# Attention loop of a four-layer kernel: up products into the ring's banks, a halved down product, a partition exchange for the rotation, and one exponential over four banks per quad

## The reference

```
xn = layernorm(x);  q = l2norm(xn @ Wq);  k = l2norm(xn @ Wk);  v = xn @ Wv
clock = softplus(xn @ clock_w + clock_b)
q = rope(q, times);  k = rope(k, times)      # r1 = x1*cos - x2*sin, r2 = x1*sin + x2*cos on channel pairs
gcp = exp(clip(cumsum(-softplus(xn @ gate_w + gate_b)), -60, 50))
q = q * gcp;  k = k / (gcp + 1e-8)
p = xn @ p_w + p_b;  p_exp = exp(p - max(p)) * clock
q = q / (cumsum(p_exp) + 1e-8);  k = k * p_exp
attn = softmax(causal(q k^T / sqrt(8)));  out = attn @ v @ out_w + out_b
x1 = out + residual;  h = layernorm(x1)
return x1 + gelu(h @ mlp_w1 + mlp_b1) @ mlp_w2 + mlp_b2
```

## Time and profile before

| what | us |
|---|---|
| median of 3 runs | 2212.62 |
| span of the profiled execution, first to last instruction | 2164.4 |
| median less span, outside the instructions | 48.2 |
| start to the first up product of step 3 | 102.7 |
| 13 steps with all parts, 41.83 each (to 646.4) | 544 |
| from 646.4 on: steps 16 to 18, then the experts, the scan and the rotation, which the change doesn't touch | 1518 |

### The profile page before, as it was taken

How to read it: one execution, slowest core, us unless ns; L and a number is a source line. 1 busy time by engine, 2 the same in 40 slices (tenths; PEclk the granted TensorE clock), 3 DMA queues, 4 the chain that set the end, 5 groups by cost and what they waited for, 6 DMA issues and landing times. The chain is left out here.

```text
span 2164.4 us, 37241 instructions
## 1 busy us (share of the span) xinstructions
PE 1849.2 (85%) x12576; PEld 954.5 (44%) x12600; DVE 1703.8 (79%) x3547; ACT 1474.7 (68%) x2917; POOL 1165.1 (54%) x720
## 2 busy tenths in 40 slices
PE   6999999999998459957889889898898988659996
PEld 2566666656665259952222222222222222124453
DVE  7778868877863437854899999999999998976776
ACT  5888888888885138845656666666666666437775
POOL 2122232242221027871789999999999998840001
PEclk9999999999999669977899999999999998879998
DMA  4100010011001012221100111001111100023333
GB/s 169 36 26 26 28 49 26 26 36 41 21 25 33 20 50 77 88 72 42 30 25 27 34 35 34 27 30 30 31 35 35 35 31 30 21 67 90 97 84 78
DMA packets 103708, 97.35 MB, mean 45 GB/s; under 512 B 9137, under 2 KB 86113, under 8 KB 103137
## 3 DMA queue, kind: packets, MB, share of 16 engines
q1 hardware_dynamic: 95584, 75.34, 12.4%
q0 software_dynamic: 6784, 18.10, 2.5%
q10 hardware_dynamic: 1152, 1.54, 0.2%
HBM read 45.87 MB, written 28.10 MB: 34 GB/s over the span
## 5 line engine op out<-in xcount | busy, mean ns | idle before, releaser
L1935 POOL TENSOR_TENSOR hc<-h,c_rep 128x1024 f32<-128x1024 f32 x256 | 627.8, 2463 | 137.9 <-DVE h L1899 136.7
L1899 DVE TENSOR_TENSOR_SCAN h<-decay,bank 128x1024 f32<-128x1024 f32 x241 | 551.0, 2286 | 22.5 <-issue 0.9
L1757 ACT ACTIVATE decay<-bank,neg_a_r 128x510 f32<-128x510 f32 x512 | 322.6, 683 | 257.5 <-PE bank L1634 257.1
L1618 PE MATMUL bank<-u_in,sel_rows 32*128 32x512 f32 x964 | 287.9, 675 | 95.7 <-DVE h L1899 95.6
L1634 PE MATMUL bank<-delta,sel_rows 32*128 32x512 f32 x1024 | 338.8, 677 | 0.9 <-ACT decay L1757 0.9
L1886 DVE TENSOR_TENSOR bank<-bank,b_rep 128x1024 f32<-128x1024 f32 x241 | 291.2, 1208 | 34.8 <-PE bank L1618 33.0
L992 POOL DMA_INDIRECT rows_in_dram<-row,idx x64 | 63.3, 989 | 318.3 <-DVE row L965 303.7
L574 ACT ACTIVATE es<-bank 128x384 f32<-128x384 f32 x512 | 208.9, 499 | 22.1 <-PE bank L373 21.8
L1618 PEld LDWEIGHTS bank<-u_in,sel_rows 32*128 32x128 f32 x964 | 76.0, 191 | 276.7 <-DVE h L1899 199.7
L1649 PE MATMUL bank<-hc,y_sel 128*32 128x512 f32 x1024 | 149.6, 660 | 0.8 <-POOL hc L1935 0.8
L1656 PE MATMUL bank<-xpad,w_conv 128*128 128x512 f32 x256 | 133.0, 634 | 3.2 <-ACT xc L1819 1.6
(11 more groups left out here) (341 smaller groups left out, 4170.0 us busy)
## 6 DMA issues: line engine op xcount, KB each, us to landing
r_tw<-r_o_t SPq DMA_DIRECT2D x96, 128.0 KB, 2.3
xvs<-xv SPq DMA_DIRECT2D x16, 512.0 KB, 2.9
u_wide<-u_rep_dram SPq DMA_DIRECT2D x30, 256.0 KB, 3.5
xs<-rows_in_dram SPq DMA_DIRECT2D x72, 68.0 KB, 1.8
front<-in_x_dram SPq DMA_DIRECT2D x16, 256.0 KB, 2.9
w<-in_w_dram SPq DMA_DIRECT2D x2, 2048.0 KB
xlb_dram<-front SPq DMA_DIRECT2D x16, 256.0 KB, 2.3
xlb_m<-xlb_dram SPq DMA_DIRECT2D x16, 256.0 KB
```

The costliest lines, as they stand in the source:

```text
L1618: last = pe.matmul(BD[n % 2][:, i * STEP:(i + 1) * STEP], sel[at:at + 32, r, :], u_in[p if n < NS else q][at:at + 32, hf, :], start=True, ...
L1757: act.activation(decay[n % 4][:, i, :, 1:], seq(DL[i])[:, :, 1:], ACT.Exp, scale=c["neg_a_r"][:, hf, g:g + 1]).then_inc(s["n_da"], 1)
L1899: dve.tensor_tensor_scan(flat(h[n % RING]), decay[n % 4].rearrange("p i b t -> p (i b t)"), flat(drive_0) if by_pool else BD[n % 2], 0.0, ...
L1935: pool.tensor_tensor(hc[n % RING][:, :, :], h[n % RING][:, :, :], c_rep[p if n < NS else q][:, :].unsqueeze(1).to_broadcast([P, 2, STEP]), ...
```

## The change

- **Up products.** `up(n)` writes bank n of the ring instead of M, and the four are issued together, behind exponential 5 of the pair at work. Quad 6 waits until all four Gelus have read the banks.
- **Down product.** It is cut in two halves of two token tiles: one ahead of quad 7, one behind weighing 6. x2 waits for the second. Weighing 7 moves behind quad 0.
- **Partition exchange.** w_qs and w_ks and their products are gone. VectorE multiplies q itself with the (signed) sine into rot_b, SP sends rot_b to rot_s with even and odd partitions swapped (`swap`, two transfers of 64 partitions), and rot minus rot_s replaces rot plus rot_b. For k the same, through the same two tiles.
- **One exponential.** `exps(n)` is one instruction over the four banks, [128 x 4 x 384], behind the last mask addition; s_score counts one for each quad.
- **Order.** On TensorE `back(3)` moves behind quad 1, `weigh(1)` behind quad 2, the transposes of xl2 and the router's product later. On ScalarE `av_copy(3)` moves behind exponential 0, `av_copy(0)` behind exponential 2, and the copy of x2t behind it. On VectorE both products of q's rotation stand ahead of x2, and the router's small steps behind `heads_o(0)`. GpSimd's L985 also waits for m_xl2.
- Start: the weights w_a come in three transfers, without the two swapped ones. `of` and `before` lie in log.

```diff
+        def swap(sp, sem):
+            for to in range(2):
+                sp.dma_start(rot_s[to:P:2, :], rot_b[1 - to:P:2, :]).then_inc(sem, 16)
...
+                sp.wait_ge(s["f_rb"], one_on)
+                swap(sp, s["f_qsw"])
+                sp.wait_ge(s["f_kb"], one_on)
+                sp.wait_ge(s["f_rq"], one_on)
+                swap(sp, s["f_ksw"])
...
-                pe.matmul(M[:, :], c["w_up"][:, n * P:(n + 1) * P], h_t[:, :], start=True, stop=True).then_inc(s["m_up"], 1)
+                pe.matmul(RING[n], c["w_up"][:, n * P:(n + 1) * P], h_t[:, :], start=True, stop=True).then_inc(s["m_up"], 1)
...
-                for st in range(HS):
-                    act.wait_ge(s["s_score"], u * 32 + HS * n + st + 1)
-                    if st == 0:
-                        since(act, s["s_av"], u * 8 + n - 1)
-                    last = act.activation(es[(n % 2) * HS + st][:, :], RING[st][:, 0:3 * P], ACT.Exp, scale=DH ** -0.5)
-                last.then_inc(s["s_exp"], 1)
+                act.wait_ge(s["s_score"], u * 8 + n + 1)
+                since(act, s["s_av"], u * 8 + n - 1)
+                act.activation(es[n % 2][:, :, :], ring[:, :, 0:3 * P], ACT.Exp, scale=DH ** -0.5).then_inc(s["s_exp"], 1)
...
+                since(dve, s["f_ksw"], 32 * k)
+                dve.tensor_tensor(seq(rot_b), seq(FA), sin, ALU.mult).then_inc(s["f_rb"], 1)
...
+                dve.wait_ge(s["f_qsw"], 32 * k + 32)
+                dve.tensor_tensor(rot[:, :], rot[:, :], rot_s[:, :], ALU.subtract).then_inc(s["f_rq"], 1)
...
                 pool.wait_ge(s["f_back"], k + 1)
+                if tail:
+                    pool.wait_ge(s["m_xl2"], k - 2)
                 pool.tensor_tensor(mag[:, 1, :], mag[:, 1, :], one_up[:, :], ALU.subtract).then_inc(s["f_lost"], 1)
```

More of the change, by code:

```diff
@@ L137, in program @@
         for name, width in W_A:
+            if name in ("w_qs", "w_ks"):
+                continue
             c[name] = c["w_a"][:, at:at + width]
@@ L165, in split3, with attention @@
     chain(dve.tensor_copy(dst[96:96 + rows], rest))
-def attention(nc, dram, d, c, banks):
+def attention(nc, dram, d, c, psum, banks):
     with ExitStack() as ctx:
@@ L275, in attention @@
         end = sb("end", [1, E])
-        of = sb("of", [1, ETILES])
-        before = sb("before", [1, ETILES])
+        of, before = (log[0:1, 0, n * ETILES:(n + 1) * ETILES] for n in range(2))
         hi = sb("p_hi", [E * FC, P], bf16)
@@ L432, in pe_step @@
                 pe.wait_ge(s["m_ht_sb"], k - 2)
-                up(0)
+                pe.wait_ge(s["s_exp"], 8 * (k - 2) + 6 if late else 8 * PAIRS)
+                for n in range(FC):
+                    up(n)
             if front:
@@ L457, in pe_step @@
                 pe.wait_ge(s["m_gelu"], 4 * k - 8)
[L458 to L462 removed]
+                down(range(0, 2))
             if late:
                 quad(7, k - 2, p)
+                weigh(6, k - 2, p)
+            if tail:
+                down(range(2, TS))
             if front:
[L466 to L470 removed]
+                pe.wait_ge(s["f_sq"], k + 1)
+                pe.wait_ge(s["f_rb"], k + 1)
+                pe.matmul(FA[:, :], c["ones_blk"], square[:, :], start=True, stop=True).then_inc(s["f_ssq"], 1)
             if k == 1:
@@ L490, in pe_step @@
                 quad(1, k - 1, q)
-            if front:
-                pe.wait_ge(s["f_mq"], k + 1)
-                project(FA, c["w_ks"], s["f_ks"])
+            if late:
+                back(3, k - 2)
             if scores:
                 weigh(0, k - 1, q)
+            if scores:
+                quad(2, k - 1, q)
+                weigh(1, k - 1, q)
             if tail:
@@ L500, in pe_step @@
                 transposes(M, xl2, s["m_x2t"])
-            if scores:
-                weigh(1, k - 1, q)
-                quad(2, k - 1, q)
-            if tail:
-                pe.wait_ge(s["m_x2t_sb"], k - 2)
-                for j in range(TS):
-                    last = pe.matmul(M[:, j * E:(j + 1) * E], o_t[:, j * P:(j + 1) * P], c["cent"][:, :], start=True, stop=True)
-                last.then_inc(s["m_aff"], 1)
             if scores:
@@ L516, in pe_step @@
             if front:
-                pe.wait_ge(s["f_ka"], k + 1)
+                pe.wait_ge(s["f_kb"], k + 1)
                 pe.wait_ge(s["f_sk"], k + 1)
                 pe.matmul(FB[:, :], c["ones_blk"], square[:, :], start=True, stop=True).then_inc(s["f_ssk"], 1)
+            if tail:
+                pe.wait_ge(s["m_x2t_sb"], k - 2)
+                for j in range(TS):
+                    last = pe.matmul(M[:, j * E:(j + 1) * E], o_t[:, j * P:(j + 1) * P], c["cent"][:, :], start=True, stop=True)
+                last.then_inc(s["m_aff"], 1)
             if scores:
@@ L599, in act_step @@
             if tail:
-                gelu(1)
+                since(act, s["m_dn"], 2 * k - 6)
+                for n in range(FC):
+                    gelu(n)
             if front:
```

163 lines of the change are left out of this document (69 added, 94 removed).

## The result

| kernel | median us | against the kernel before, same chip |
|---|---|---|
| before | 2212.77 (2210.34 to 2213.51) | |
| changed | 2288.47 (2275.89 to 2295.76) | 1.0341 [1.0305, 1.0377] |

The change costs 76 us, 3.4%. The forecast was 62 us more, 2275. The direction and the place were right, the size was somewhat too small; 2288 lies within the range of 2238 to 2305.

A forecast was written before the change was run, and what follows sets the result against it. It took TensorE to bound the attention-loop step, with about 2 us of gaps. 13 steps x 5.0 = 65, less 3 at the ends, gave 62 on top of 2212.6: 2275 us, range 2238 to 2305.

The forecast's parts named there:

- The walk through the step: One attention-loop step followed wait by wait from its first up product: 46.8 us, 5.0 us longer.
- The 13 steps: The 13 steps of the attention loop, each 5.0 us longer: 65 us.
- rival 1: TensorE's clock drops after the new gaps ahead of quads 1 and 2: 7.2 us a step, 2303; chance 0.2.
- The ends: Steps at the loop's ends: last -4, two before it +1 each, two without a tail and the first -1 together.
- the part that treats the exchange alone: Removed and added work in a step: TensorE's work falls by 1.9 us, the exchange's transfers are hidden and cost nothing.
- The gain in the last step: Last step, only the tail left: three up products no longer wait out their Gelus, about -4 us.
- The 48.2 us outside the span: Time around the profiled 2164.4 us span, up to the median of 2212.6, said not to change: 48.2 us.
- The ping-pong: Up products alternating with Gelus ahead of the down product: its removal buys 0.15 us, 8.8 against 8.96.
- The premise: Attention-loop step bound by TensorE, busy 39.88 of 41.83 us, with about 2 us of gaps.
- Rival 2: TensorE stays the attention step's bound and the kernel gets faster: step 38.9 us, -38 in all, 2175; chance 0.1.

The follow-up runs named there:

- the second profile of the kernel before: The kernel before, unchanged, profiled again: 2209.43 us, span 2207.3, a loop step of 43.2 us except the first.
- the faster variants: The kernel before with up products in the ring and GpSimd's two products waiting for m_xl2: 2180.93 us, 0.9867.
- the last of these runs: The changed kernel with whole down product ahead of quad 7, variances vv3 ahead of the read of back 3, avs copy 0 ahead of exponential 2: 2261.75 us, 1.0214.

## Why the prediction was right, and where its size was off

**The step.** The walk through the step held. Counted from the first up product of the step at 115.02, with the forecast in brackets: x2 14.60 (15.2), m_ln 16.65 (17.2), exponential 0 19.13 (19.6), the read of back 3 22.56 (23.05), the Ln of m_vv 22.94 (23.4), exponential 1 24.90 (25.4), quad 2 26.39 (26.9), xl2 25.00 (25.5), exponential 2 29.16 (29.7), quad 3 33.99 (33.9), next step 46.80 (46.8). The wait of ScalarE ahead of m_ln, forecast at 3.5, is 3.63; quad 1 waits 1.57 (1.7), weighing 0 0.83 (0.8), quad 2 2.18 (2.4). The one exponential takes 1.44 us (1.45). The exchange lands in 2.1 us (2.3) and holds nobody in a full step. Xl2 takes 1.11 and the clip 1.31 (1.03 and 1.10).

That 46.80 is met so closely is in part luck. From x2 to exponential 2 everything comes some 0.5 us earlier than forecast. From the transposes back (L412, 146.32) to quad 3 (149.01) it then takes 2.69 us, part of it at the low clock, where 2.2 were forecast without it; in the last of the 13 steps, at full clock, the same stretch takes 2.24 (735.64 to 737.88). The two errors cancel at quad 3.

By the Trainium skill, page "SBUF — State Buffer", section "Who interferes with whom", a VectorE instruction with two SBUF inputs and a GpSimd one that reads SBUF hold each other up. The trace of the exchange alone agrees at a new place: the small product L854, of two SBUF inputs and 8 columns, took 1.25 us there beside GpSimd's mag (352.78 to 354.11), while in the changed kernel, where GpSimd waits for xl2, it took 0.16 (at 139.94), and 0.17 in the profile before (at 416.60).

**Terms that were off.** Against the second profile of the kernel before (span 2207.3) the changed kernel's (2291.7) is 84.4 us longer; the medians differ by 76. Of these 11.7 lie before the first up product of step 3 (115.02 against 103.34), 77.6 in the 13 steps (636.24 against 558.6), 1.8 in the next two, and -6.7 behind.

1. *The 13 steps, 65 forecast, 77.6 measured.* The chain is 5.0 in the first, 4.4 in the last and 5.3 on average in the eleven between, once the extra of five long steps is taken off: 67. That extra is rival 1, the clock, which was given 0.2 and as a thing that happens or not. It happens in every step but the last, and costs little in most. In the step at 115.02 the clock falls at quad 2, and the transposes (L412) and ssk that follow run at half speed; but the transposes back wait anyhow for exponential 2 and the copy behind it, and quad 3 comes at 33.99 instead of the 33.9 forecast. Of the 2.2 us of the rival only the half us told above is left; the rest was already paid for by the chain. In every second of the steps from the fourth on it falls some 5 us later, behind a wait for the avs copy, and the slow stretch lies on quad 3 itself:

```profile
388.96 0.66 PE L412 MATMUL bank<-consts,avs 128*128 128x128 f32 x4 [1.90 <-ACT avs L585]
389.45 1.66 PE L522 MATMUL bank<-square,consts 128*128 128x512 f32 x2
390.91 1.71 PE L526 MATMUL bank<-cent,o_t 128*128 128x8 f32 x8
392.55 1.24 PE L378 MATMUL bank<-q_t,k_m 32*128 32x256 f32 x8
```

   These steps take 50.55 instead of 48.52; five of them make 10 us.

2. *The ends, -3 forecast, +6.8 measured.* I gave the two steps without a tail a gain of 1.9 us of projections each. They pay for the exchange instead: alone it delays the first up product of step 3 by 5.5 us; all parts in the old order delay it by 6.7 (110.04 against 103.34), and the order by the other 5.0. It is the same mistake as in the part that treats the exchange alone, where its subtraction was called "as many VectorE instructions as before". The number is the same, the place is not: it stands ahead of xl2. The gain in the last step, put at 4, was too small by half: from its first up product to the end of its down product the changed kernel takes 9.82 us (837.20 to 847.02) instead of 18.62, 8.8 less. Some 2 us in the later stages, which the change doesn't touch, make up the rest.

3. *The 48.2 us outside the span.* This step was wrong. The profiled execution was shorter than the timed ones by the stalls at the seams (1.36 each) and by 28.7 us in the experts' stage, not by anything around it, which is 2.1 us. The sum was made as a difference, so this didn't cost the forecast anything.

4. *The ping-pong "has bought 0.15 us".* It buys 0.6: the down product starts 8.17 us into the changed step, not 8.8 (quad 6 starts 0.3 earlier than forecast, and from it to the down product are 3.47 us, not 3.8), and in the run with the ups alone it makes each step 0.6 shorter, somewhat less than half of that run's 1%. In the changed kernel the rest of the chain was late enough to bury it.

**The premise.** "The step is bound by TensorE, with about 2 us of gaps" was half of it. TensorE is nearly gapless there and yet 1.9 us less of work brings nothing (1.0107 alone, +0.7 us a step on top of the faster variants). Rival 2 rested on that premise and was rightly given little. The forecast itself didn't need it, since it followed each wait.

**What stays open.** Which place in the new order costs how much. Undone one at a time or together, the places gave back 0.4 to 1.3 points of 4.4, and the next wait took over each time. In the last of these runs the wait left is on the read of back 3, at 21.0 us of the step against 19.0 with all parts in the old order. Quad 3 comes at 31.0 against 27.6, so the read accounts for 2.0 of 3.4 us at most. The other 1.4 lie behind it: in the new order the router's product (L524) waits for a copy on ScalarE behind exponential 2 and stands with the transposes back ahead of quad 3 (429.06), while in the old order it ran ahead of them (345.60). Both are read from the rows; neither place was run by itself. What the stall of 1.36 us at the seams is stays open too.

## What to carry to other kernels

A step whose engines hand over to each other is priced by walking it through, instruction by instruction, with all that is queued behind each wait; that gave the first step's length to 0.1 us, with errors of half a us that cancelled, where the busy table alone would have said "faster". Before work is taken from the busiest engine, look what its largest remaining gap waits for: if another chain ends within a microsecond, only work on that chain counts, and an instruction moved onto it costs its full length. A change of several parts and an order is best run part by part: here the ups in the ring and one added wait on GpSimd were worth 1.3%, and the new order lost three times that.

## What the runs showed of the hardware

- Clock. In the steps of the kernels whose longest wait of TensorE in mid-step was 0.4 to 1.1 us (up to 1.5 in the last of the 13) the granted clock stayed at 1.00. In the exchange alone, with a wait of 2.24 us, it fell in 6 of 13 steps (to a mean of 0.96, 1.3 us longer). In the changed kernel and its variants, with waits of 1.5 to 2.7 us, it fell in most steps (0.86 to 0.96; 2.2 us longer in the last variant, 47.37 against 45.19). The longest wait alone doesn't decide it: steps of one kernel with the same wait, 2.24 us in one and 2.68 in another, ran both with and without the fall.
- One activation over four banks, [128 x 4 x 384], takes 1.44 us, against 1.62 to 1.64 for four of 384 columns one behind the other.
- Two executions of the kernel before differed by 43 us of 2207 in span, with a granted clock of 1.00 in the loop in both. A term like "time outside the span" needs a second profile.
